# Reordering the first loads of a two-layer attention kernel and spreading its late loads

## The reference, cut to what matters

```
x = x + tanh(g_xattn[0]) * attn0(layernorm(x), ctx)     # 16 heads of 16, biases, time bias -0.1*|t-s|, output projection
x = x + tanh(g_ffn[0])   * ffn0(layernorm(x))           # weights quantised to -1, 0, 1; relu
x = x + tanh(g_xattn[1]) * attn1(layernorm(x), ctx)     # relu on q, k, v; no bias
x = x + tanh(g_ffn[1])   * moe1(layernorm(x))           # 4 experts, argmax router, gelu, final layernorm
```

## Time and profile before

| | |
|---|---|
| median of 3 runs | 740.31 us (739.7 to 742.17) |
| profiled execution, its time | 741.31 us |
| its span | 739.5 us |
| PE busy | 691.2 us (93%) |
| DVE busy | 567.0 us (77%) |
| ACT busy | 453.1 us (61%) |
| POOL busy | 368.8 us (50%) |
| moved by DMA | 87.56 MB |

### The profile page before, as it was taken

The page is one execution under the profiler, slowest core; times in us unless marked ns, Lnnn a source line. Parts: engine busy times, 40 slices in busy tenths (PEclk is TensorE's granted clock), DMA queues, the critical chain, the costliest instruction groups (busy, mean ns, idle before and its releaser), DMA issues.

```text
span 739.5 us, 12829 instructions
## 1 busy us (share of the span) xinstructions
PE 691.2 (93%) x4390; PEld 434.9 (59%) x4390; DVE 567.0 (77%) x1037; ACT 453.1 (61%) x972; POOL 368.8 (50%) x442
## 2 busy tenths in 40 slices
PE   7886999999999899999999999999999899999993
PEld 5654444444443588788663444444444688999983
DVE  6786899999993267575888999999997667666673
ACT  3413888888888464856316888888887324333330
POOL 4641566565555433864500022645662756665543
PEclk9998999999999999999999999999999999999998
DMA  5898645555545434003134455432201432211100
GB/s 184 273 252 220 204 148 178 185 152 181 178 168 217 137 97 132 26 1 101 43 104 121 124 156 180 130 97 78 78 2 60 120 127 73 66 38 44 34 9 16
DMA packets 51423, 87.56 MB, mean 118 GB/s; under 512 B 8661, under 2 KB 16855, under 8 KB 51360
## 3 DMA queue, kind: packets, MB, share of 16 engines
q1 hardware_dynamic: 43184, 71.39, 31.1%
q0 software_dynamic: 4640, 11.54, 5.6%
q10 hardware_dynamic: 3536, 3.81, 2.0%
HBM read 44.92 MB, written 41.63 MB: 117 GB/s over the span
## 4 chain that ended last, share of the span: by engine, by line
PE 59%; POOL 10%; issue 9%; DVE 8%; SPq 5%; DMA 5%; ACT 2%; POOLq 0%; another core or an unknown queue 0%; DVEq 0%; ACTq 0%
PE ps_out L856 10%; PE ps_wide L1053 6%; PE ps_out L1076 6%; PE ps_wide L725 6%; PE ps_a L839 6%; SPq L517 3%; PE ps_a L978 3%; PE ps_misc L839 3%; POOL w_lo L1377 3%; PE ps_a L635 2%; PE ps_a L1065 2%; DMA stack_q<-planes_q 2%; PE ps_out L992 2%; PE ps_wide L652 2%; PE ps_misc L992 1%
## 5 line engine op out<-in xcount | busy, mean ns | idle before, releaser
L1688 DVE TENSOR_REDUCE row_max<-ps_wide 128x2 f32<-128x1024 f32 x256 | 301.7, 1220 | 21.1 <-PE ps_wide L725 20.3
L1199 ACT ACTIVATE probs<-ps_a 128x512 f32<-128x512 f32 (+1 forms) x418 | 199.1, 522 | 28.6 <-PE ps_a L839 26.7
L725 PE MATMUL ps_wide<-stack_k,stack_q 48*128 48x512 f32 x512 | 145.1, 470 | 11.6 <-DVE row_max L1688 4.3
L839 PE MATMUL ps_a<-stack_q,stack_k 62*128 62x512 f32 (+3 forms) x418 | 137.3, 391 | 2.1 <-ACT probs L1199 1.5
L856 PE MATMUL ps_out<-probs,vals 128*17 128x512 f32 x1024 | 134.1, 598 | 0.5 <-POOL probs L1455 0.5
L1199 ACT ACTIVATE probs<-ps_misc 128x512 f32<-128x512 f32 (+1 forms) x222 | 114.0, 514 | 16.5 <-PE ps_misc L839 13.8
L1455 POOL TENSOR_TENSOR probs<-probs,fixes_sb 128x512 f32<-128x512 f32 x64 | 82.2, 1284 | 79.1 <-ACT probs L1199 79.1
L839 PEld LDWEIGHTS ps_a<-stack_q,stack_k 62*128 62x128 f32 (+1 forms) x418 | 63.5, 184 | 67.4 <-ACT probs L1199 30.9
L725 PEld LDWEIGHTS ps_wide<-stack_k,stack_q 48*128 48x128 f32 x512 | 68.4, 184 | 47.0 <-DVE row_max L1688 26.2
L839 PE MATMUL ps_misc<-stack_q,stack_k 62*128 62x512 f32 (+3 forms) x222 | 87.8, 396 | 1.3 <-ACT probs L1199 1.2
L839 PEld LDWEIGHTS ps_misc<-stack_q,stack_k 62*128 62x128 f32 (+1 forms) x222 | 40.9, 184 | 39.1 <-ACT probs L1199 30.4
(11 more groups left out here) (288 smaller groups left out, 1413.1 us busy)
## 6 DMA issues: line engine op xcount, KB each, us to landing
rows_sorted<-blank SPq DMA_DIRECT2D x17, 1040.0 KB, 5.0
planes_k<-planes SPq DMA_DIRECT2D x32, 256.0 KB, 3.7
planes_q<-planes SPq DMA_DIRECT2D x32, 256.0 KB, 3.8
stack_k<-planes_k SPq DMA_DIRECT2D x64, 128.0 KB, 2.9
stack_q<-planes_q SPq DMA_DIRECT2D x64, 128.0 KB, 2.8
w_raw<-in_L_W SPq DMA_DIRECT2D x6, 1024.0 KB, 5.3
stack_k<-planes_k SPq DMA_DIRECT2D x64, 64.0 KB, 2.6
stack_q<-planes_q SPq DMA_DIRECT2D x64, 64.0 KB, 2.7
```

Source lines behind the costliest of these rows:

```text
L725: mm(raw_slot(l, ("pair", g, p))[:, i * S:(i + 1) * S], stack_q[at, slot(g, c) + q * P:slot(g, c) + (q + 1) * P], stack_k[at, slot(g, c):s ...
L839: mm(score_slot(("tile", n))[:, start:end], stack_k[at, slot(g, c) + k * P:slot(g, c) + (k + 1) * P], stack_q[at, slot(g, c) + start:slot( ...
L1199: do(probs[n % PROBS[l]][:, j, start:end], score_slot(("tile", n * TILES + t))[:, start:end], ACT.Exp, scale=0.25).then_inc(exp_done, 1)
L1688: v.tensor_reduce(row_max[:, g % 2, :, p], raw_slot(l, ("pair", g, p))[:].rearrange("p (i k) -> p i k", i=2), AX, ALU.max).then_inc(sem(f" ...
```

## The change

The nine first loads get another order and finer semaphores: w_k, context 0, x 0, w_v, ident, w_q, the biases of q and k, bias_v. The copy to `w_v_hi` goes from DVE to ACT. ACT issues `load_inputs(1)` after its copies. Four of the seven loads of `load_rest` (w_o, bias_2, b1_cols, order) and the three weight loads of layer 1 are issued by SP in groups 0 to 3. The constant rows are copied in two parts: POOL fills 3 periods instead of 7, and SP, after store q3 and ahead of group 3's stacks, copies the first four periods to the other four in four transfers. In `FIRST_RAWS` pair 0 moves from after the queries of batch 2, half 0, to after the values of batch 2, second pair, and each later pair up to 4 moves on by one.

```diff
-FIRST_RAWS = {(2, "q", 0): (0, 2), (2, "q", 1): (2, 2),
-              (3, "k", 0): (4, 2), (3, "k", 1): (6, 1), (3, "v", 0): (7, 1), (3, "v", 1): (8, 2),
+FIRST_RAWS = {(2, "v", 1): (0, 1), (2, "q", 0): (1, 2), (2, "q", 1): (3, 2),
+              (3, "k", 0): (5, 1), (3, "k", 1): (6, 1), (3, "v", 0): (7, 1), (3, "v", 1): (8, 2),
...
+            for signal, dst, src in (
+                (loaded_keys, w_qkv["k"][:], part(a["L0_Wk"])),
+                (loaded_context, *context_in(0)),
+                (loaded_rows, *rows_in(0)),
+                (loaded_values, w_qkv["v"][:], part(a["L0_Wv"])),
+                (loaded_rest, ident[:], a["ident"]),
+                (loaded_queries, w_qkv["q"][:], part(a["L0_Wq"])),
+                (loaded_rest, bias_qk[:, 0, :], a["L0_bq"]),
+                (loaded_rest, bias_qk[:, 1, :], a["L0_bk"]),
+                (loaded_rest, bias_v[:], a["L0_bv"].partition_broadcast(P)),
             ):
+                sp.dma_start(dst, src).then_inc(signal, 16)
...
                     store_planes("q", 3)
+                    sp.wait_ge(sem("rows_in0"), 16 * 2 * N_ATT)
+                    sp.wait_ge(loaded_rest, 16 * (N_FIRST + N_REST))
+                    for i in range(2):
+                        for rows in constant_rows(i):
+                            sp.dma_start(rows[:, RING * S:].bitcast(F32), rows[:, 0:RING * S].bitcast(F32)).then_inc(loaded_rest, 16)
                     load_stacks(RING - 1)
...
                     sp.wait_ge(sem("vals_done0"), T // 2)
-                    for s_ in "kvq":
-                        sp.dma_start(w_qkv[s_][:], part(a[f"L1_W{s_}"])).then_inc(sem("w_layer1"), 16)
+                    later = tuple((w_qkv[s_][:], part(a[f"L1_W{s_}"])) for s_ in "kvq") + (
+                        (w_o[:], part(a["L0_Wo"])), (bias_2[:], a["L0_b2"].partition_broadcast(P)), (b1_cols[:], a["L0_b1"]), (order[:], a["order"]))
...
+                    if l == 0 and g < QT:
+                        for dst, src in later[max(2 * g - 1, 0):2 * g + 1]:
+                            sp.dma_start(dst, src).then_inc(loaded_context, 16)
...
+                    if (l, g, k, t) == (0, RING // 2, 0, 0):
+                        pe.wait_ge(loaded_rest, 16 * (N_FIRST + N_REST + N_ATT))
...
-            act.wait_ge(loaded_keys, 16 * N_KEYS)
...
-            load_inputs(1)
+            act.wait_ge(loaded_context, 16)
             for c in range(C):
                 do(ctx_hi[:, c, 0:S], context_of(0)[:, c, :], ACT.Copy).then_inc(sem("parts_high"), 1)
+            act.wait_ge(loaded_values, 16)
+            do(w_v_hi0[:], w_qkv["v"][:], ACT.Copy).then_inc(sem("parts_high"), 1)
+            load_inputs(1)
+            act.wait_ge(loaded_rest, 16 * N_FIRST)
...
-                    (w_o[:], part(a["L0_Wo"])), (gates_raw[:], a["gates"].partition_broadcast(P)),
-                    (bias_o[:], a["L0_bo"].partition_broadcast(P)), (bias_2[:], a["L0_b2"].partition_broadcast(P)),
-                    (b1_cols[:], a["L0_b1"]), (fixes[:], a["fixes"]), (order[:], a["order"]),
+                    (gates_raw[:], a["gates"].partition_broadcast(P)), (fixes[:], a["fixes"]),
+                    (bias_o[:], a["L0_bo"].partition_broadcast(P)),
...
-                    if l == 0 and g == QT:
+                    if l == 0 and g == QT + 1:
                         weights_split("k")
...
-                            pool.dma_start(rows[:, S:].rearrange("r (n t) -> r n t", t=S),
-                                           rows[:, 0:S].unsqueeze(1).broadcast_to([n, RING * 2 - 1, S])).then_inc(sem("rows_in0"), 16)
+                            pool.dma_start(rows[:, S:RING * S].rearrange("r (n t) -> r n t", t=S),
+                                           rows[:, 0:S].unsqueeze(1).broadcast_to([n, RING - 1, S])).then_inc(sem("rows_in0"), 16)
...
-            dve.wait_ge(loaded_values, 16 * N_VALUES)
-            v.tensor_copy(w_v_hi0[:], w_qkv["v"][:]).then_inc(sem("parts_low"), 1)
-            dve.wait_ge(sem("parts_low"), C + 3)
+            dve.wait_ge(sem("parts_high"), C + 1)
             weight_low("v")
             normal(0, 0, x)
-            dve.wait_ge(sem("parts_high"), C + 1)
+            dve.wait_ge(sem("parts_high"), C + 2)
             weight_low("q")
+            dve.wait_ge(loaded_rest, 16 * N_FIRST)
```

More of the change, by code:

```diff
@@ L368, in gated_blocks_program @@
         loaded_rest = sem("loaded_rest")
-        N_KEYS, N_VALUES, N_ROWS, N_IN, N_REST, N_ATT = 4, 3, 2, 2, 7, 4
+        loaded_context, loaded_queries = sem("context0_then_layer1"), sem("queries0_then_ffn0")
+        N_FIRST, N_IN, N_REST, N_ATT = 4, 2, 3, 4
         block = ctx.enter_context(nc.Block())
@@ L440, in planes_left, with constant_rows @@
                 wait(eng, sem(f"planes_kept{l}_{i}"), 2 * 16 * ((n - i + UNITS - 1) // UNITS))
+        def constant_rows(i):
+            return (stack_q[HALF * i + KS + MP:HALF * i + KS + MP + NB, :], stack_k[HALF * i + KS:HALF * i + KS + MP + NB, :])
         def rows_in(b):
@@ L467, in _ @@
         def _(sp):
[L468 to L473, removed]
-            ):
-                for dst, src in moves:
-                    sp.dma_start(dst, src).then_inc(signal, 16)
+            for signal, dst, src in (
[8 more added lines that the diff above has]
+                (loaded_rest, bias_v[:], a["L0_bv"].partition_broadcast(P)),
+            ):
+                sp.dma_start(dst, src).then_inc(signal, 16)
             def load_last(n):
@@ L589, in _ @@
                     sp.wait_ge(sem("normalised0"), G)
-                    sp.dma_start(w1_raw[:], part(a["L0_W1"])).then_inc(sem("w_ffn0"), 16)
-                    sp.dma_start(w2_raw[:], part(a["L0_W2"])).then_inc(sem("w_ffn0"), 16)
+                    sp.dma_start(w1_raw[:], part(a["L0_W1"])).then_inc(loaded_queries, 16)
+                    sp.dma_start(w2_raw[:], part(a["L0_W2"])).then_inc(loaded_queries, 16)
             for i in range(LANDING):
@@ L643, in values @@
                 if v == 0 and l == 0:
-                    pe.wait_ge(sem("parts_low"), C + 4)
+                    pe.wait_ge(sem("parts_low"), C + 3)
                 elif v == 0:
@@ L902, in turn_n0 @@
             def turn_n0(b):
+                if b == 0:
+                    pe.wait_ge(loaded_rest, 16 * N_FIRST)
                 pe.wait_ge(sem("normed"), QT * (b + 1))
@@ L942, in _ @@
             pe.wait_ge(sem("exp_done0"), G * QT * TILES)
-            pe.wait_ge(sem("w_layer1"), 16 * 3)
+            pe.wait_ge(loaded_context, 16 * (1 + 7))
             pe.wait_ge(sem("normalised0"), G)
@@ L1243, in _ @@
                 if b == 0:
[L1244 removed]
+                    act.wait_ge(loaded_queries, 16)
                     do(w_q_hi0[:], w_qkv["q"][:], ACT.Copy).then_inc(sem("parts_high"), 1)
@@ L1256, in _ @@
                     load_rest()
-            act.wait_ge(loaded_rest, 16 * N_REST)
+            act.wait_ge(loaded_rest, 16 * (N_FIRST + N_REST))
             do(gates[:], gates_raw[:], ACT.Tanh).then_inc(sem("gates"), 1)
@@ L1274, in _ @@
                 if b < 2:
-                    act.wait_ge(sem("w_ffn0"), 32)
+                    act.wait_ge(loaded_queries, 16 * 3)
                     wait(act, sem("abs_sum"), b)
@@ L1488, in attention @@
                             expert_weights(*divmod(n, QT))
-            def constant_rows(i):
-                return (stack_q[HALF * i + KS + MP:HALF * i + KS + MP + NB, :], stack_k[HALF * i + KS:HALF * i + KS + MP + NB, :])
             for i in range(2):
@@ L1499, in _ @@
                 if b == 0:
-                    pool.wait_ge(sem("parts_low"), C + 5)
+                    pool.wait_ge(sem("parts_low"), C + 4)
                 keys_low(0, b)
@@ L1897, in _ @@
             v.memset(vals[:, :, :, DH:VW], 1.0)
-            dve.wait_ge(loaded_keys, 16 * N_KEYS)
+            dve.wait_ge(loaded_keys, 16)
             def weight_low(s_):
@@ L1944, in _ @@
                     normal(0, b + 1, x)
-            dve.wait_ge(loaded_rest, 16 * N_REST)
+            dve.wait_ge(loaded_rest, 16 * (N_FIRST + N_REST))
             attention(0)
```

11 lines of the change are left out of this document (4 added, 7 removed).

## The result

The kernel after takes 742.31 us (median of 20 runs, 740.12 to 745.24) beside 740.33 us before (20 runs, 738.13 to 742.17): a ratio of 1.0025, 95% interval 1.0015 to 1.0035. The forecast was 736.7 with a range of 734.0 to 740.4, so the time lies above the range, 5.6 us from the forecast. It is slower by less than the 0.3% that the prediction called "the same", and slower than no change by the interval. The profiled execution took 742.79 us, 740.8 of it span.

A forecast was written before the change was run, and what follows sets the result against it. PE was taken as bound in attention, with gains only before 84 us, chiefly its 3.9 us wait for group 1's stacks. Terms -1.6 + 1.9 - 3.9 - 1.4 + 1.1 + 0.3 = -3.6 us gave a median of 736.7, range 734.0 to 740.4.

The forecast's parts named there:

- the clock term: Last query projection, behind pair 8: without the wait for group 1's stacks PE's clock stays up, 1.4 us gained.
- The third rival: Pair 0: its new wait brings PE's clock down, slowing the projection of batch 2; 739.6 us, chance 0.07.
- Start, -1.6: First loads: reordered loads and finer semaphores bring `w_q_lo` to 12.45 instead of 14.02, 1.6 us gained.
- Pair 0, +1.9: Before pair 8: early pair 0 waits 2.6 us for group 0's stacks, making DVE and PE 1.9 us later.
- Group 1's stacks, -3.9: Ahead of pair 8: less traffic from POOL's copies and late loads removes PE's whole 3.9 us wait.
- SP's copies, +1.1: Before group 1's maxima: four copies add 2.6 us, three weight loads leaving save 1.5; 1.1 us lost.
- Late loads, +0.3: Groups 0 to 3: loads moved there delay the next maxima, 0.3 us lost, range 0 to 1.5.
- Stacks in time: Pair 0: group 0's stacks land in time, so the 1.9 us loss goes; 734.8 us, chance 0.15.
- the wait on group 1 stays: Pair 8: SP's own traffic keeps the stack wait and half clock; 740.1 us, halfway cases 738, chance 0.20.
- The copies clog SP's queue: SP's queue before group 3's stacks: copies take 10.6 us instead of 2.6; 744.7 us, slower, chance 0.08.

The follow-up runs named there:

- e2: Kernel after, with SP's four copies issued around the first sending of maxima, where SP was idle; pair 0 stays early: 740.21 us, 1.0001 of before.
- e5: Kernel after, with four matmuls on zeros filling PE's wait ahead of the early pair 0: 741.10 us, 1.0006 of before.
- e10: e8 with the q and k biases loaded ahead of w_v and bias_v on a semaphore only DVE waits for: 736.82 us, 0.9936 of before.
- e4: Kernel before, with only the reordered first loads of the change: 739.27 us, 0.9987 of before.
- e6: Kernel before, with only the new order of pairs (pair 0 a step sooner): 740.46 us, 1.0003 of before.
- e1: Kernel after, with pair 0 and pairs 1 to 4 back in their old places: 739.61 us, 0.9989 of before.
- e7: Kernel after, with all constant rows copied by POOL as before and none by SP: 740.05 us, 0.9995 of before.
- e3: Kernel after, with pairs back in their old places and SP's copies moved to its idle time: 736.73 us (7 runs), 0.9952 of before.
- e11: e3 repeated on another chip with more runs: 737.76 us, 0.9955 of before.
- e8: Kernel after, with pairs back, SP's copies in its idle time and the seven late loads one a group in groups 2 to 8: 739.08 us, 0.9964 of before.
- e9: Kernel after, with four matmuls on zeros ahead of the early pair 0 and SP's copies in its idle time: 737.73 us, 0.9964 of before.

## Why the prediction was wrong

**What failed** is the clock term: "Without that wait PE's clock should stay up", with its 1.4 us of gain. Behind pair 8 it did: the six matmuls of the last query projection ran at full clock. But the sum let the new waits idle PE at no cost to the clock. The third rival, "the new wait costs the clock", had a chance of 0.07 and a time of 739.6, and it came true twice: behind pair 0's wait, which I had computed (2.6 us, measured 2.07), and behind the wait for the maxima, which I had made longer by 1.1 us without seeing that it becomes a wait of the same length as the other. The first cost 1.7 us (12.47 from pair 0 to `newton` against 10.73 at full clock, e2), the second about 1.2 (from group 1's first score to the next load 10.97 us against 9.80 before). The rival's own 739.6 is still 2.7 below the measured time, so it was not the whole.

In the profiles the kernel after is 2.2 us behind at the end of group 3, where the sum has it 3.6 ahead. The sum had 5.0 us of lead at the last query plane (-1.6 + 1.9 - 3.9 - 1.4), and 1.54 were there: 1.7 of the missing 3.5 are the clock behind pair 0, and most of the rest is the shorter gain of the start and the 2.0 us in which POOL held DVE. Of this last the prediction has half: it says that ACT's key outputs, coming sooner, "no longer hold POOL", but gives no price to POOL's then running beside DVE. Behind the last query plane another 2.3 us are missing: 0.7 in the wait for the maxima, 1.2 in the clock behind it and about 0.4 in group 3.

The mean granted clock over all runs points the same way for the medians. A mean clock c means that (1 - c) times the span is lost to the clock, if PE is the bound: 0.0148 x 740.8 = 11.0 us after. For the kernel before, the runs beside the experiments had means of 0.9878, 0.9890 and 0.9875, which make 8.1 to 9.2 us. By this estimate the clock costs the kernel after 1.7 to 2.8 us more, which is as much as the 2.0 us between the medians. It is rather too high, since PE is not the bound in every half-clock stretch, and e5 shows how far it can be off: its mean of 0.9902 is 0.0050 above the 0.9852 of the kernel after, 3.7 us by the estimate, and its ratio is lower by 0.0019, 1.4 us. All eleven experiments have a higher mean clock than the kernel after and a lower ratio, but e5, with a clock above that of the kernel before beside it (0.9890), is no faster than that kernel. So the clock is a large part of the loss and not all of it.

**The other steps,** by the terms of the sum:
- *Start, -1.6.* The right mechanism, mis-sized: 0.5 at `w_q_lo`, 1.15 at batch 1's keys. bias_v was assumed to land at 9.3 and landed at 10.52, 5.48 us after an issue at 5.04 that I had put at 4.7. e10 shows that it would not have helped to be right there: with bias_v out of the way DVE's chain ends at 13.57, not at my 12.0, which had `ctx_lo` come 2.0 us sooner; it came 0.85 sooner (6.58 against 7.43). PE's first projection stood at 7.30 and not at 6.9, since the warm-up matmuls took 6.05 us instead of 5.31. e4, the start alone, is 0.9987 (0.9968 to 1.0007): the medians do not show a gain.
- *Pair 0, +1.9.* The wait was right (2.07 for 2.6). Its price by itself, e6, is nothing that shows; with ACT's loads out of the way it is the 0.36% of e1, 2.7 us. PE came to pair 8 at 60.63 us. The forecast was 58.7 less the 1.6 of the start, so 57.1, and 60.71 is what the kernel before has: up to there nothing had been gained.
- *Group 1's stacks, -3.9.* Right in the trace: no wait, and 3.13 us of issues for "3 to 4 us". I had put 63 of the 112 engine-us to POOL's copies and 49 to ACT's loads. By e7 the former were not needed: with POOL's copies at their old length the wait is gone too. Whether ACT's loads were is open, since e6 has them as before and no wait.
- *SP's copies, +1.1.* Undersized: 3.3 us from 71.62 to 74.95 for 2.6, each issue 0.72 to 0.87 where I took 0.65 between bounds of 0.43 and 0.73. The wait for the maxima is 1.97 us where the kernel before has next to none (group 1 starts at 84.15 and 83.84, from leads of 1.5 and 0), so 1.8 net. The upper bound was not one: it was the issue of another shape. The larger error was the place. e2, e3 and e11 issue the same copies 10 us earlier, where SP has nothing to do, and there they cost nothing that the trace shows.
- *Late loads, +0.3.* 0.6 us of wait in group 3; e8 removes it, and its time does not tell.

**The rivals.** "Stacks in time" and "the wait on group 1 stays" did not happen. "The copies clog SP's queue" did not either: 3.3 us, far from its 8.4. On the rule of the Trainium skill that I weighed (DMA: Bandwidth & Descriptors, "Rules for kernel authors", an outermost dimension under 16 confines a transfer to as many engines), no run tells: the copies' landing isn't in the records, and group 2, the first to need them, did not wait in the kernel after. Its sister rule in the Trainium skill (the same page, "Issuing engines are not separate DMA queues"), that transfers issued by different engines run on the same 16 DMA engines and interleave, agrees with e7, where POOL's longer copies go with SP issues of 7.74 us instead of 3.13.

**What stays open.** Why a wait of 2.07 us was followed by 0.56 of the clock, and ones of 1.76 (e2, then 1.00), 2.36 (e7, then 0.76) and 2.53 (e6, then 0.76) by more. How often POOL's key planes meet DVE's normalisation, and what that costs the medians: each version has one profile, and there DVE loses 2.0 us in the kernel after, 2.15 in e5, 1.0 to 1.1 in e2, e8 and e10, and nothing in the others. The Trainium skill (TensorE: Matmul & The Clock Gate, "What's actually happening") says that the count of slow matmuls at a kernel's start varies from run to run; the 7.8 us spread of e2 is of that kind, though not at the start. Whether e10 is truly better than e3 is open too.

## What to carry to other kernels

A wait of PE costs its own length and then, in some executions, the clock behind it; so two waits of 2 us can be dearer than one of 4, and a forecast must price each new wait with and without the clock, even if it makes another one vanish. When a change lets one engine start sooner, look at what will then run beside it: here POOL's planes came sooner and met DVE's normalisation. Put work that an in-order queue must issue where that queue is idle: the same four copies cost some 0.35% between the last stores and the next loads, and nothing that a trace shows 10 us earlier. Before moving work ahead of a wait, ask when its inputs land; starting pair 0 a step sooner only moved PE's idle time to where nothing could fill it. Where idle time can't be avoided, matmuls on a blank tile are worth a try, though e5 and e9 do not show a gain clear of noise.

## What the runs showed of the hardware

- PE's clock is a lottery at such waits: the same instructions up to 57 us had 0.56 from 42 to 49 us in one profile and 1.00 in another, and the runs of e2 spread over 7.8 us with it. What the half clock cost there was 0.75 us at 0.76 and 1.74 at 0.56 (from pair 0 to `newton`).
- It needs no wait for a transfer. In e8 and e11 the clock fell to 0.52 and 0.53 from 67 to 73 us, after 5.11 of 7 us busy (e8). In e2 the same place, with the same load ahead of it (5.12 of 7), had the full clock:

```profile
60.00:67.00 7.00, 5.12 (x21) 2.61 (x21) 5.94 (x9) 1.47 (x3) 0.00 (x0) 1.00 0.78 167
```

```profile
67.00:73.00 6.00, 5.61 (x24) 1.96 (x22) 5.80 (x6) 4.11 (x10) 1.79 (x4) 1.00 0.72 223
```

- Copies within SBUF on POOL's queue lengthen the issue of SP's transfers, not only their landing: four issues take 2.92 us with none in flight (at 31.73 in the kernel before), 3.13 with 18% of the engines on that queue, 3.81 with 27%, 4.14 with 34% and 7.74 with 68%.
- DVE lost time beside POOL's elementwise instructions (`planes<-full,planes`, 1.28 us each): a `newton` step of 0.17 us took 1.16 and ended with POOL's, and the four-instruction normalisation took 1.38 us with none beside it, 2.34 to 2.48 with one inside it (after, e2, e8, e10), and 3.53 with two (e5). Where POOL's began in DVE's last 0.4 us (e1, e3, e9), DVE kept its 1.38 and POOL's took 1.46 to 1.51.
